# The running sum over tiles in two expert routings: from VectorE's doubling steps to accumulating products of TensorE

## The reference

```python
router_logits = x_flat @ gate_w
router_probs = jax.nn.softmax(router_logits, axis=-1)
expert_idx = jnp.argmax(router_probs, axis=-1)
expert_w = jnp.take_along_axis(router_probs, expert_idx[:, None], axis=1)[:, 0]
for e in range(NUM_EXPERTS):
    h = jax.nn.gelu(x_flat @ w1[e] + b1[e], approximate=False)
    y = h @ w2[e] + b2[e]
    out = out + jnp.where(expert_idx == e, expert_w, 0.0)[:, None] * y
```

## Time and profile before

| | |
|---|---|
| median of 3 runs | 1849.13 us (1848.25 to 1849.85) |
| the profiled execution | 1851.53 us |
| its span, first to last instruction | 1849.7 us |
| TensorE (PE) busy | 1609.4 us, 87%, 9990 products |
| VectorE (DVE) busy | 1070.8 us, 58%, 3025 instructions |
| ScalarE (ACT) busy | 906.8 us, 49% |
| GpSimd (POOL) busy | 379.6 us, 21% |

### The profile page before, as it was taken

One profiled execution on the slowest core, in us unless ns is written; L12 is line 12 of the kernel. 1 busy time (PEld: TensorE's weight loads), 2 busy tenths in 40 slices (PEclk: granted clock), 3 DMA queues, 4 the chain that ended last, 5 costly groups with the idle time before them and its releaser, 6 DMA issues.

```text
span 1849.7 us, 27965 instructions
## 1 busy us (share of the span) xinstructions
PE 1609.4 (87%) x9990; PEld 1215.6 (66%) x9998; DVE 1070.8 (58%) x3025; ACT 906.8 (49%) x2034; POOL 379.6 (21%) x480
## 2 busy tenths in 40 slices
PE   6999858999669999999958699999998779995566
PEld 5677637889556676767535667776675468894444
DVE  7767752222356666666667765555555534325887
ACT  4888821222136666666539455555554102223366
POOL 1000014111132323233240100000000342223734
PEclk9999989999879999999978899999999889997878
DMA  9000028889500000000000200000000338893001
GB/s 339 2 1 1 2 92 322 260 291 292 170 1 12 7 7 7 7 1 1 1 1 1 80 12 7 7 7 7 1 1 12 129 124 264 300 352 127 0 12 35
DMA packets 61625, 152.26 MB, mean 82 GB/s; under 512 B 8960, under 2 KB 39696, under 8 KB 55248
## 3 DMA queue, kind: packets, MB, share of 16 engines
q1 hardware_dynamic: 54096, 133.91, 21.9%
q0 software_dynamic: 5280, 14.47, 2.0%
q10 hardware_dynamic: 2112, 2.10, 0.4%
HBM read 133.89 MB, written 24.75 MB: 86 GB/s over the span
## 4 chain that ended last, share of the span: by engine, by line
PE 69%; DVE 15%; ACT 5%; POOL 4%; issue 4%; DMA 2%; POOLq 1%; SPq 0%; DVEq 0%; ACTq 0%
PE bank L1033 8%; PE bank L1456 8%; PE bank L976 8%; PE bank L1510 7%; PE bank L1523 6%; PE bank L1497 5%; PE bank L1460 5%; PE bank L1440 3%; PE bank L679 3%; PE bank L1862 2%; POOL sorted_h L1225 2%; PE bank L695 2%; PE bank L710 1%; ACT p1f L1578 1%; PE bank L616 1%
## 5 line engine op out<-in xcount | busy, mean ns | idle before, releaser
L1707 DVE TENSOR_REDUCE small<-bank 128x1 f32<-128x512 f32 x128 | 82.5, 686 | 108.7 <-PE bank L1510 108.7
L1052 ACT ACTIVATE e2a<-bank,WB 128x128 f32<-128x128 f32 x156 | 44.6, 368 | 178.7 <-PE bank L1033 178.7
L1703 DVE CUSTOM_DVE_ANT_0 p1f<-bank,p1f 128x512 f32<-128x512 f32 x128 | 83.2, 687 | 81.3 <-PE bank L1510 81.3
L1581 ACT ACTIVATE p2f<-bank,small 128x512 f32<-128x512 f32 x128 | 86.9, 683 | 86.2 <-DVE small L1707 86.1
L751 ACT ACTIVATE l<-l,small 128x256 f32<-128x256 f32 x256 | 108.9, 502 | 32.6 <-DVE small L817 32.2
L1578 ACT ACTIVATE p1f<-p1f,small 128x512 f32<-128x512 f32 x128 | 91.2, 714 | 67.9 <-DVE small L1703 67.5
L400 POOL TENSOR_SCALAR rs<-mv 128x4 f32<-128x4 f32 x16 | 3.6, 226 | 567.4 <-DVEq L230 551.7
L817 DVE CUSTOM_DVE_ANT_0 l<-bank,small 128x256 f32<-128x256 f32 x256 | 90.7, 420 | 13.4 <-PE bank L695 12.5
L1456 PE MATMUL bank<-WA,HT 128*128 128x256 f32 x384 | 93.1, 387 | 5.0 <-DVE p1f L1648 5.0
L1592 ACT ACTIVATE p2f<-bank 128x512 f32<-128x512 f32 x128 | 75.2, 598 | 40.5 <-PE bank L1497 39.0
L1052 ACT ACTIVATE e0a<-bank,WB 128x128 f32<-128x128 f32 x128 | 36.6, 368 | 112.7 <-PE bank L1033 112.7
(11 more groups left out here) (402 smaller groups left out, 3949.6 us busy)
## 6 DMA issues: line engine op xcount, KB each, us to landing
WB<-in_L2pack SPq DMA_DIRECT2D x39, 514.0 KB, 5.1
WB<-in_L2pack SPq DMA_DIRECT2D x39, 512.0 KB, 5.7
WB<-in_L0pack SPq DMA_DIRECT2D x16, 1028.0 KB, 6.4
WB<-in_L0pack SPq DMA_DIRECT2D x16, 1024.0 KB, 7.3
e0a<-in_L0pack SPq DMA_DIRECT2D x7, 1028.0 KB, 5.8
e0a<-in_L0pack SPq DMA_DIRECT2D x7, 1024.0 KB, 6.8
sorted_h<-in_blank SPq DMA_DIRECT2D x6, 1032.0 KB, 16.1
e2a<-sorted_h SPq DMA_DIRECT2D x39, 129.0 KB, 5.6
```

Of the source, the lines that this page charges most:

```text
L1581: ins = a.e.activation(P, k.bank(x), ACT.Exp, bias=self.mx[:, m:m + 1], accum_out=self.sm[:, m:m + 1])
```

## The change

`counted` becomes a flag with two events. The ones product goes first, into bank 6, and raises it. The triangle product starts an accumulation in bank 7, and n - 1 ones products follow into the same bank, the s-th reading the first n - s tiles and adding them to the columns from tile s on. So each tile of bank 7 ends as `pre` plus the totals of all earlier tiles; the last product raises the flag again. VectorE sums the totals over the tiles from bank 6 (all tokens of each expert), works out the blocks from that, waits for the second event only before it adds the block bases, and reads the running sum from bank 7 there.

```diff
--- before.py
+++ after.py
@@ -897,7 +897,7 @@
         self.ag = [k.dma(f"gather{i}", 1) for i in range(4 * topk)]
         f = k.flag
         nq = self.nq = nf // 4
-        self.logits, self.counted, self.exped = f("e_logits", 1), f("e_counted", 1), f("e_exped", 1)
+        self.logits, self.counted, self.exped = f("e_logits", 1), f("e_counted", 2), f("e_exped", 1)
         self.lt, self.ltc = f("turned", 4), f("pt", 4)
         self.two = topk == 1
         if self.two:
@@ -917,8 +917,11 @@
             other.first_pe(t)
         bk, n = k.bank(7), self.n
         t.wait_ge(self.routing, self.SELECTED)
-        t.e.matmul(bk[:, 0:8 * n], k.trib[:, :], self.selb, start=True, stop=True)
-        t.e.matmul(bk[:, 256:256 + 8 * n], k.onesbb[:, :], self.selb, start=True, stop=True).then_inc(self.counted.sem, 1)
+        t.e.matmul(k.bank(6)[:, 0:8 * n], k.onesbb[:, :], self.selb, start=True, stop=True).then_inc(self.counted.sem, 1)
+        t.e.matmul(bk[:, 0:8 * n], k.trib[:, :], self.selb, start=True, stop=False)
+        for s in range(1, n):
+            ins = t.e.matmul(bk[:, 8 * s:8 * n], k.onesbb[:, :], self.selb[:, 0:8 * (n - s)], start=False, stop=s == n - 1)
+        ins.then_inc(self.counted.sem, 1)
         for other in self.beside:
             other.next_pe(t)
         if self.two:
@@ -1105,21 +1108,11 @@
         k, e, n, nt, I, nb = self.k, v.e, self.n, self.nt, self.I, self.nb
         Mf = self.M.rearrange("p c t e -> p (c t) e")
         e.tensor_copy(self.selb, Mf.rearrange("p t e -> p (t e)")).then_inc(self.routing.sem, 1)
+        pre = k.bank(7)[:, 0:8 * n].rearrange("p (t e) -> p t e", e=8)
+        all_of, exc = I[0][:, 0, :], I[1]
         v.wait_ge(self.counted, 1)
-        bk = k.bank(7)
-        pre = bk[:, 0:8 * n].rearrange("p (t e) -> p t e", e=8)
-        tot = bk[:, 256:256 + 8 * n].rearrange("p (t e) -> p t e", e=8)
-        v.chain(e.tensor_copy(I[0], tot))
-        cur, s = 0, 1
-        while s < n:
-            o, i = I[1 - cur], I[cur]
-            e.tensor_tensor(o[:, s:n, :], i[:, s:n, :], i[:, 0:n - s, :], ALU.add)
-            v.chain(e.tensor_copy(o[:, 0:s, :], i[:, 0:s, :]))
-            cur, s = 1 - cur, s * 2
-        inc, exc = I[cur], I[1 - cur]
-        v.chain(e.tensor_tensor(exc, inc, tot, ALU.subtract))
-        v.chain(e.tensor_tensor(exc, exc, pre, ALU.add))
-        v.chain(e.tensor_scalar(nb[0], inc[:, n - 1, :], 63.5, 1.0 / 128, ALU.add, ALU.mult))
+        v.chain(e.tensor_reduce(all_of, k.bank(6)[:, 0:8 * n].rearrange("p (t e) -> p e t", e=8), AX.X, ALU.add))
+        v.chain(e.tensor_scalar(nb[0], all_of, 63.5, 1.0 / 128, ALU.add, ALU.mult))
         v.chain(e.tensor_scalar(nb[0], nb[0], MAGIC, MAGIC, ALU.add, ALU.subtract))
         v.chain(e.tensor_copy(nb[1], nb[0]))
         cur, s = 1, 1
@@ -1131,7 +1124,8 @@
         T = nb[cur]
         v.chain(e.tensor_tensor(nb[0], T, nb[0], ALU.subtract))
         v.chain(e.tensor_scalar(nb[0], nb[0], 128.0, None, ALU.mult))
-        v.chain(e.tensor_tensor(exc, exc, nb[0].rearrange("p (o e) -> p o e", o=1).to_broadcast([128, n, 8]), ALU.add))
+        v.wait_ge(self.counted, 2)
+        v.chain(e.tensor_tensor(exc, pre, nb[0].rearrange("p (o e) -> p o e", o=1).to_broadcast([128, n, 8]), ALU.add))
         v.chain(e.tensor_tensor(exc, exc, Mf, ALU.mult))
         v.chain(e.tensor_reduce(self.posf, exc, AX.X, ALU.add))
         e.tensor_copy(self.pos, self.posf).then_inc(self.routing.sem, 1)
```

## The result

The changed kernel takes 1844.86 us, the median of 20 runs (1841.94 to 1851.03), and the kernel before on the same chip 1850.51 us (20 runs, 1845.32 to 1855.25). The ratio is 0.9974, 95% interval 0.9965 to 0.9982: 4.8 us less, between 3.3 and 6.5. The medians lie 5.65 apart and the means 5.00, with a standard error of 0.85; 5.67 were forecast. The kernel before takes about 1851 us in some measurements and about 1875 in others, on one and the same chip too, and in the traces of the changed kernel 24 of these 25 us lie between the counting and the first GELU of the two routings (54.9 against 71.9 us in e2, 24.5 against 31.8 in e0), so each kernel is compared with runs of before that were taken beside it.

A forecast was written before the change was run, and what follows sets the result against it. The prediction took VectorE's chain of small dependent instructions in both routings as the bound: 2.26 + 3.57 - 0.16 = 5.67 us less, from 1849.13 to 1843.5 us, with 8 in 10 for 1841.3 to 1846.8.

The forecast's parts named there:

- VectorE, e0: First routing stage: one 128-column sum from PSUM replaces L1112 to L1121 on VectorE; 2.26 us gained.
- VectorE, e2: Second routing stage: one 256-column sum from PSUM replaces the five doubling steps; 3.57 us gained, 3.41 after waiting.
- TensorE in time: Running sum from TensorE's narrow products, 0.07 us floor each: VectorE waits 0.16 us in e2, none in e0.
- Rival (a): The accumulating products bind: at 0.12 us each, e2 waits 1.45 and e0 0.3; 4.1 us gained, 1845.0; chance 0.13.
- What stands behind: Key and value products queued on TensorE behind e2's products end near 1459.0, before VectorE wants them at 1459.3; no cost.
- Passing on: Behind both routings the gain gets through: 3.41 us pass in e2, and e0's masks, gathering and loads move together.
- rival (b): Gain mostly given back behind e0 by clock, strided sum, products and weight loads: 2.5 to 3.5 gained, 1846.3; chance 0.16.
- The clock: TensorE's half clock at e0's gathering, L956: between 1.8 us gained and 1.1 lost; taken as 0.
- rival (d): More gain: the clock does not fall in e0, gaining 1.8 us, 1841.7; chance 0.10.
- The slower rival (c): More of the span at half clock: gain gone from 11.3 us more, 1853.5 with 20 us more; chance 0.07.
- The signs: In the after trace: sum 0.29 and 0.42 us, wait at most 0.16, L956 2.3 earlier, e2's L1018 5.7 earlier.

The follow-up runs named there:

- again_more: The changed kernel unaltered, measured a third time as reference for three delay and repeat kernels, against the kernel before (1875.65 us): 1870.15 us, ratio 0.9975.
- the filled kernel: Changed kernel plus 40 unread ones products of 128 columns behind e0's counting products: 1845.81 us, ratio 0.9972 to the kernel before.

## Why the prediction was right

- **VectorE, e0.** Forecast 2.26, measured 2.20, and 2.25 where the first counting product ran at full clock as before. The strided sum cost what a contiguous pass of its size cost, 0.30 us in e0 and 0.43 in e2. Right.
- **VectorE, e2.** Forecast 3.57, measured 3.57 in the trace. Right.
- **TensorE in time.** Right that it comes in time; the size was off. I took 0.07 us as the floor for narrow products and charged 0.16 us of waiting. In the trace the last five of them, of 40 to 8 columns, start 0.025 us apart, and the wait was 0, with 0.45 us to spare, so e2 gained 3.57 and not 3.41. Their weight loads did not bind either: each of the 31 has one, of 0.10 us in its own record, 3.0 us in all, and the 31 products took 1.94 us. Rival (a) falls.
- **What stands behind.** The keys and values (L2069) began at 1448.86 and ended at 1452.56; the four additions that take them out still took 2.46 us, without a wait. Right.
- **Passing on.** This is the term that was sized too well. In e2, 3.53 of 3.57 us reached the turning of the sorted rows and 3.3 to 3.4 the last GELU. In e0 all of the 2.20 reached L959, 1.83 the issue of the third block's load, and 1.2 the last GELU, as that load took 9.03 and 9.15 us where it had been 8.43. I had written that it moves together with the rest and put nothing for it; rival (b) had this loss, though not its size. By the ratios, the three comparisons of the change with before measure 4.8, 4.1 and 4.7 us, each interval holding 5.77; pooled, my means give 4.7 with an error of 0.5. That agrees with the 4.5 to 4.6 at the ends of the two stages, so about a us of what the routings save does not arrive, and the traces place it in e0. The pair of one-stage kernels has 0.8 of the 2.2 at the last GELU of e0. But the traces of e0 also scatter (`again_more` needs 216.4 us there, the kernel with the new e0 alone 213.5), so the exact size is not settled. Nor is the slope: ten us put back twice arrived nearly whole, six us as one to two.
- **The clock.** I took 0 between a gain of 1.8 and a loss of 1.1. In the profiled execution L959 ran at half clock for 4.3 us rather than 3.7, and the gathering took 0.36 longer. In the two kernels with filler TensorE stands still for 0.85 and 0.45 us ahead of the gathering, where it was 4.3 and 4.7 in the changed kernels beside them; their gathering has no half clock and takes 14.1 us in place of 16.2 and 16.8. In the filled kernel that is 2.1 us less. In the trace of the filled kernel the scatter's landing takes these back; in the runs (1.0 less, error 1.0) this is not decided. So whether rival (d), had the clock stayed up, would have given its 1.8 stays open.
- **The slower rival (c).** Single executions do differ by more than the change, and with the clock (of the 20 runs the fastest, 1841.94, has a mean clock of 0.946, the slowest, 1851.03, has 0.941), but evenly for both kernels: mean granted clock 0.9412 before and 0.9420 after in the comparison with 35 and 12 runs. My argument against (c), that the three runs of before differed by 1.6 us, was weak: 20 runs of it differ by 9.9.
- **The signs.** The addition from PSUM did not wait, and the sum took 0.30 and 0.43. The two starts that I named on the span's own time did not come as written: L956 was to start 2.3 us earlier and the turning in e2 5.7; they started 3.6 and 9.4 earlier, and the end was 6.7 earlier. The clock ahead of and between the stages had moved them. Counted from each stage's first counting product it is 2.2 and 3.53. A shift on the span's time was the wrong thing to name.

That the medians lie 5.65 apart, beside 5.67 forecast, is luck: the runs scatter by 2.4 and 3.0 us (one standard deviation), the means of the same runs lie 5.0 apart, and the best estimate of all comparisons is 4.7.

## What to carry to other kernels

Where a chain of small dependent VectorE instructions is awaited, each costs its start-to-start time (here about 0.2 us for 8 columns and 0.46 for 256), and a linear step of it (a running sum, a shift, a total) can go to TensorE as a row of accumulating narrow products, as long as the row ends before the instructions that VectorE keeps. Order the products so that the one needed first is issued first, and place the wait at the reader, not at the head. When a change is worth less than the scatter of single executions, prove its length in the trace and its sum in many runs of both kernels on one chip; and when a wait is filled to lift the clock, look whether a DMA behind it was the next in line.

## What the runs showed of the hardware

- Accumulating bf16 products into one PSUM bank, with overlapping columns and a weight load each, start 0.025 us apart at full clock when they have 40 columns or fewer (e2, and e0 in the filled kernel), and 0.11 apart at 248. At half clock (e0, changed kernel) it is 0.027 at 24 and 16 columns, 0.041 at 40 and 0.10 at 120.
- Ones products of 128 columns in a row, each with its weight load (the fillers), start 0.107 us apart at half clock and 0.056 at full.
- A reduction on VectorE that reads PSUM at a stride of eight f32 words took 0.29 us for 128 columns and 0.42 for 256, as the contiguous passes do.
- With the products four times over the mean granted clock was higher than in the changed kernel (0.9455 against 0.9420, and 0.9412 against 0.9389), and the time was longer, not shorter. The mean clock alone is no measure of a kernel.
- A delay of 5 us or more ahead of e2's scatter left TensorE at full clock from the first to the last GELU of e2, in four traces of four; in ten without it the clock was at half for 3.4 to 6.8 us there, and the stretch was 1 to 3 us longer.
